# A decoder layer on one core: the end of the cross attention's norm moves from GpSimd to VectorE

## The reference

```
x = x + xattn(layernorm(x), ctx)
q, k, v = relu(query @ Wq + bq), relu(ctx @ Wk + bk), relu(ctx @ Wv + bv)   # 16 heads of 16
probs   = softmax(causal(q k^T / 4))
out     = probs @ v + q
xattn   = (out - mean(out)) * rsqrt(var(out) + 1e-5) * gamma + beta
```

## Time and profile before

| | us |
|---|---|
| median of 3 runs | 1577.68 (1575.25 to 1577.74) |
| the profiled execution, its own time | 1575.13 |
| its span | 1573.4 |
| mean granted clock of TensorE | 0.972 of full speed |

### The profile page before, as it was taken

One profiled execution on the slowest core, in us unless ns is written; L12 is line 12 of the kernel. 1 busy time (PEld: TensorE's weight loads), 2 busy tenths in 40 slices (PEclk: granted clock), 3 DMA queues, 4 the chain that ended last, 5 costly groups with the idle time before them and its releaser, 6 DMA issues. The chain is left out here.

```text
span 1573.4 us, 55175 instructions
## 1 busy us (share of the span) xinstructions
PE 1472.8 (94%) x21214; PEld 1069.1 (68%) x21214; DVE 1085.3 (69%) x3026; ACT 890.6 (57%) x1542; POOL 869.5 (55%) x1172
## 2 busy tenths in 40 slices
PE   5999999999999999986999999999999759999997
PEld 3777777777777777765777677777767536666664
DVE  5667777776767777644566666666666548988986
ACT  2555555555555555543656566665656427777773
POOL 1455555555555455541667776777777724454453
PEclk8999999999999999988999999999999959999998
DMA  5400000000000000003000000000000000000001
GB/s 157 131 2 1 0 0 0 0 0 0 0 0 0 0 0 0 2 2 116 20 19 13 20 13 20 13 17 17 13 20 8 2 1 21 28 34 33 27 34 40
DMA packets 31205, 32.37 MB, mean 21 GB/s; under 512 B 3937, under 2 KB 29602, under 8 KB 31138
## 3 DMA queue, kind: packets, MB, share of 16 engines
q1 hardware_dynamic: 31138, 31.46, 6.5%
HBM read 23.06 MB, written 8.39 MB: 20 GB/s over the span
## 5 line engine op out<-in xcount | busy, mean ns | idle before, releaser
L994 POOL TENSOR_SCALAR_AFFINE_SELECT a_probs_t<-a_probs_t 128x512 f32<-128x512 f32 x256 | 161.8, 666 | 84.1 <-ACT a_probs_t L676 84.1
L1475 DVE TENSOR_REDUCE c_neg_max<-score_banks 128x8 f32<-128x512 f32 (+1 forms) x128 | 116.7, 953 | 101.5 <-PE score_banks L1247 101.4
L1587 POOL TENSOR_SCALAR_AFFINE_SELECT c_probs_t<-c_probs_t 128x512 f32<-128x512 f32 x256 | 153.2, 634 | 34.2 <-ACT c_probs_t L1401 34.1
L1008 POOL TENSOR_TENSOR a_less<-a_attn,a_remote 128x512 f32<-128x512 f32 x32 | 40.7, 1273 | 226.7 <-DVE a_attn L854 226.7
L362 PE MATMUL side_banks<-a_xn_t,a_w_qk 128*128 128x256 f32 x512 | 134.1, 397 | 1.8 <-ACT a_xn_t L621 1.8
L1401 ACT ACTIVATE c_probs_t<-score_banks 128x2048 f32<-128x2048 f32 x64 | 120.3, 1880 | 25.9 <-PE score_banks L1275 25.9
L676 ACT ACTIVATE a_probs_t<-score_banks 128x2048 f32<-128x2048 f32 x64 | 120.2, 1878 | 25.7 <-PE score_banks L520 25.7
L831 DVE TENSOR_REDUCE a_neg_max<-score_banks 128x8 f32<-128x512 f32 (+1 forms) x128 | 116.4, 951 | 13.9 <-PE score_banks L488 13.9
L362 PEld LDWEIGHTS side_banks<-a_xn_t,a_w_qk 128*128 128x128 f32 x512 | 93.4, 197 | 11.7 <-ACT a_xn_t L621 2.2
L2090 POOL TENSOR_TENSOR r_hn<-rz_t,half_hn 128x256 f32<-128x256 f32 x32 | 23.3, 729 | 123.6 <-ACT rz_t L1922 123.6
L631 ACT ACTIVATE a_k_z<-side_banks,a_b_k,row_half 128x256 f32<-128x256 f32 x128 | 61.7, 562 | 47.4 <-PE side_banks L362 47.4
(11 more groups left out here) (255 smaller groups left out, 3939.8 us busy)
## 6 DMA issues: line engine op xcount, KB each, us to landing
x_sb<-in_x SPq DMA_DIRECT2D x32, 256.0 KB, 2.9
c_ctx_in<-in_ctx SPq DMA_DIRECT2D x32, 256.0 KB, 2.7
out<-y SPq DMA_DIRECT2D x32, 256.0 KB, 2.1
w_ih<-in_ffn_w_ih SPq DMA_DIRECT2D x1, 768.0 KB, 6.5
w_hh<-in_ffn_w_hh SPq DMA_DIRECT2D x1, 768.0 KB, 7.3
a_raw_qk<-in_attn_qk_w SPq DMA_DIRECT2D x1, 512.0 KB, 3.6
a_raw_cross<-in_xattn_qk_w SPq DMA_DIRECT2D x1, 512.0 KB, 4.4
b_ih<-in_ffn_b_ih SPq DMA_DIRECT2D x1, 384.0 KB, 6.6
```

What stands on the lines that cost most here:

```text
L994: nc.gpsimd.affine_select(out=probs, in_=probs, pattern=[[0, 4], [1, 128]], compare_op=ALU.is_ge, fill=0.0, base=-1, channel_multiplier=-1 ...
L1475: ins = nc.vector.tensor_reduce(neg_max[:, tt, :].rearrange("p (i s l) -> p i s l", i=4, s=2)[:, :, :, late], all_scores[:, :, :, 128 * (1 ...
L1587: nc.gpsimd.affine_select(out=heads, in_=heads, pattern=[[0, 4], [1, 128]], compare_op=ALU.is_ge, fill=0.0, base=0, channel_multiplier=-1) ...
```

## The change

`out_scale` no longer writes normed, but ends the norm itself: two instructions with three operands (subtract the mean, times gamma) write scaled, and, once `add_beta` and these are done, two more (times one over the deviation, plus x_beta) write x. GpSimd loses `scale_normed`; it gets `add_beta(old)`, one instruction that writes x + beta into the new tile x_beta, between `out_deviation(old)` and `x_deviation(second)`. The tiles normed and shifted go; `add_query` waits for scaled instead of normed.

```diff
             def out_scale(at):
                 dve.wait_ge(norm_scaled, at.count(1, 1))
-                wait(dve, x_done, at.count(1, 0))
-                norm_scale(lambda tt: summed[:, tt, :], normed, out_moments, out_rstd, norm_ready)
+                for tt in range(2):
+                    ins = nc.vector.scalar_tensor_tensor(scaled[:, tt, :], summed[:, tt, :], out_moments[:, tt, 0:1],
+                                                         cross.gamma[:], ALU.subtract, ALU.mult)
+                ins.then_inc(scaled_ready, 1)
+                dve.wait_ge(beta_added, at.count(1, 1))
+                dve.wait_ge(scaled_ready, at.count(1, 1))
+                for tt in range(2):
+                    ins = nc.vector.scalar_tensor_tensor(x_rows(at, tt), scaled[:, tt, :], out_rstd[:, tt:tt + 1],
+                                                         x_beta[:, tt, :], ALU.mult, ALU.add)
+                ins.then_inc(x_done, 1)
...
             def add_query(at):
-                wait(pool, norm_ready, at.count(1, 0))
+                wait(pool, scaled_ready, at.count(1, 0))
...
-            def scale_normed(at):
-                pool.wait_ge(norm_ready, at.count(1, 1))
-                nc.gpsimd.tensor_tensor(scaled[:], normed[:], cross.gamma[:].unsqueeze(1).to_broadcast([128, 2, D]),
-                                        ALU.mult).then_inc(shift_step, 1)
-                pool.wait_ge(shift_step, at.count(2, 1))
-                nc.gpsimd.tensor_tensor(shifted[:], scaled[:], cross.beta[:].unsqueeze(1).to_broadcast([128, 2, D]),
-                                        ALU.add).then_inc(shift_step, 1)
-                pool.wait_ge(shift_step, at.count(2, 2))
-                nc.gpsimd.tensor_tensor(x_pair(at), x_pair(at), shifted[:], ALU.add).then_inc(x_done, 1)
+            def add_beta(at):
+                wait(pool, x_done, at.count(1, 0))
+                nc.gpsimd.tensor_tensor(x_beta[:], x_pair(at), cross.beta[:].unsqueeze(1).to_broadcast([128, 2, D]),
+                                        ALU.add).then_inc(beta_added, 1)
 
             def step(at):
...
                 if old.real:
                     mask_weights(old, 1)
-                if older.real:
-                    scale_normed(older)
                 if old.real:
                     add_query(old)
                 if prev.real:
                     mask_weights(prev, 0)
                 if old.real:
                     out_deviation(old)
+                    add_beta(old)
                 if second.real:
                     x_deviation(second)
```

More of the change, by code:

```diff
@@ L1112, in cross_attention @@
     summed = sb("summed", [128, 2, D])
-    normed = sb("normed", [128, 2, D])
     scaled = sb("scaled", [128, 2, D])
-    shifted = sb("shifted", [128, 2, D])
+    x_beta = sb("x_beta", [128, 2, D])
     k_bank, q_bank, av_bank, back_bank = bank[4:8]
@@ L1132, in cross_attention @@
     sum_step, attn_ready, sum_ready = s("sum_step"), s("attn_ready"), s("sum_ready")
-    norm_step, norm_eps, norm_scaled, norm_ready = s("norm_step"), s("norm_eps"), s("norm_scaled"), s("norm_ready")
-    shift_step, x_done, pool_turn = s("shift_step"), s("x_done"), s("pool_turn")
+    norm_step, norm_eps, norm_scaled, scaled_ready = s("norm_step"), s("norm_eps"), s("norm_scaled"), s("scaled_ready")
+    beta_added, x_done, pool_turn = s("beta_added"), s("x_done"), s("pool_turn")
     pe_turn = s("pe_turn")
@@ L1592, in add_query @@
                 pool.wait_ge(qT_ready, at.count(1, 1))
-                wait(pool, norm_ready, at.count(1, 0))
+                wait(pool, scaled_ready, at.count(1, 0))
                 nc.gpsimd.tensor_tensor(summed[:], attn[:], q_tok[at.par][:], ALU.add).then_inc(sum_ready, 1)
-            def scale_normed(at):
-                pool.wait_ge(norm_ready, at.count(1, 1))
-                nc.gpsimd.tensor_tensor(scaled[:], normed[:], cross.gamma[:].unsqueeze(1).to_broadcast([128, 2, D]),
-                                        ALU.mult).then_inc(shift_step, 1)
-                pool.wait_ge(shift_step, at.count(2, 1))
-                nc.gpsimd.tensor_tensor(shifted[:], scaled[:], cross.beta[:].unsqueeze(1).to_broadcast([128, 2, D]),
-                                        ALU.add).then_inc(shift_step, 1)
-                pool.wait_ge(shift_step, at.count(2, 2))
-                nc.gpsimd.tensor_tensor(x_pair(at), x_pair(at), shifted[:], ALU.add).then_inc(x_done, 1)
+            def add_beta(at):
+                wait(pool, x_done, at.count(1, 0))
+                nc.gpsimd.tensor_tensor(x_beta[:], x_pair(at), cross.beta[:].unsqueeze(1).to_broadcast([128, 2, D]),
+                                        ALU.add).then_inc(beta_added, 1)
             def step(at):
-                prev, old, older, second = at.back(), at.back(2), at.back(3), at.back(-2)
+                prev, old, second = at.back(), at.back(2), at.back(-2)
                 if old.real:
                     mask_weights(old, 1)
-                if older.real:
-                    scale_normed(older)
                 if old.real:
```

## The result

The changed kernel takes 1618.13 us (median of 4 runs, 1617.58 to 1619.69) against 1576.47 us before (1575.00 to 1577.74) in the same comparison: 41.7 us more, ratio 1.0269 (95% interval 1.0255 to 1.0283). The forecast was 1610, the sum behind it +32.9 us.

A forecast was written before the change was run, and what follows sets the result against it. It took TensorE, waiting for GpSimd's second masks in cross attention, to bound the kernel: 37.1 us of waits less 4.2 at the stage's end gave 1608.0, with the median's 2.55 more 1610.6; forecast 1610 us, range 1602 to 1621.

The forecast's parts named there:

- the sum: Cross-attention stage: 37.1 us of added TensorE waits less 4.2 us at the stage's end, +32.9 us.
- The main step: add_beta in GpSimd's queue ahead of the second masks makes TensorE wait 1.25 us more a period, about 17.45 us.
- The part prices: Last pairs of the stage: pair 29 pays 0.82 us for add_beta, pair 30 the full 1.25 us.
- The clock: Rival: TensorE's idle time lowers its clock for a tenth of its stage work, some 51 us more, 1661; 6%.
- the prediction's signs of being wrong: Period of 16.2 to 16.6 us, transposed scores waiting for VectorE instead of masks, or granted clock under 1.00.
- the range: Whole kernel: 1602 us (1.0 us a period) to 1621 us (both upper bounds).
- the room above 1610: Contention and addresses at their bounds: 0.13 + 0.23 us more a period, +10 us, 1620; 7% for either at full size.
- VectorE's part: Four out_scale instructions ahead of row_max take 1.6 to 1.7 us, 0.9 more, costing nothing under GpSimd's delay.
- The rival itself: VectorE decides and GpSimd's delay is swallowed: 0.15 to 0.35 us a period, 1578 to 1584 us; 4%.
- Contention: GpSimd's masks meeting VectorE's small instructions on the maxima: bounds 0 and 0.13 us a period, taken as 0.
- the end of the stage: After the last pair's attn, add_query starts earlier and the shorter norm ends sooner: 4.2 us less.
- The row that the prediction named for it: VectorE's c_xn at 978 ns where GpSimd is busy, beside 0.73 us for a pair of the same form.

The follow-up runs named there:

- Experiment 2: Kernel before plus one unused 128x512 GpSimd instruction between out_deviation and x_deviation, VectorE unchanged: 1614.93 us, ratio 1.0264.
- 1: Changed kernel with add_beta(old) moved right behind add_query(old), no longer between the deviations: 1579.46 us, ratio 1.0036.
- 7: Kernel before plus one unused GpSimd instruction of half size (128x256) between out_deviation and x_deviation: 1594.12 us, ratio 1.0128.
- experiment 8: Kernel before plus two unused 128x512 GpSimd instructions between out_deviation and x_deviation: 1687.50 us, ratio 1.0711.
- experiment 3: Changed kernel with four extra transposes of ident on TensorE in its wait ahead of the second half's values: 1612.48 us, ratio 1.0236.
- experiment 10: Kernel before plus two unused 128x512 GpSimd instructions and twelve extra TensorE transposes in the wait for the masks: 1652.86 us, ratio 1.0492.
- 9: Changed kernel with add_beta behind add_query and x_deviation one step later, behind the second masks; out_scale whole at its place: 1581.75 us, ratio 1.0042.
- experiment 4: Changed kernel with add_beta behind add_query, x_deviation behind the second masks, out_scale at the end of VectorE's step: 1565.05 us, ratio 0.9937.
- experiment 5: Kernel before, arithmetic untouched, with only x_deviation moved one step later, behind the second masks: 1555.21 us, ratio 0.9887.

## Why the prediction was right, and where its sizes were off

*The main step held to the hundredth.* The queue of GpSimd between the moments and the second masks closes a loop through TensorE, and `add_beta` in it costs 1.24 us of every period: the forecast period of 17.45 us is the one measured. Experiment 2 has it with nothing else changed, 1 takes it away by moving one line, 7 and 8 scale it (16.90 and, in the undisturbed periods, 18.69). The part prices are right too. From the opening of a step to its second block of mask matmuls, between which the waiting matmuls of `values` sit, pair 29 takes 3.84 us before and 4.66 after, 0.8 more (0.82 predicted), and pair 30 takes 3.39 and 4.61, 1.2 more (1.25 predicted). The waits are thus 34.7 + 0.8 + 1.2 = 36.7 us, against 37.1 in the sum.

*The clock was the term that the sum lacked.* It stood among the rivals, as a fall for a tenth of the stage at 51 us. It came in addition, and small: five falls of 1.5 us in the profiled execution, 7.5 of the 10 us by which its span grew more than the sum said (43.0 against 32.9). One of the prediction's signs of being wrong, a granted clock under 1.00 in the stage, did show. That the result still lies in the range is in part luck: the room above 1610 stood there for contention and addresses, which cost nothing in the loop, and the clock filled it. Experiments 3 and 10 show the cause: TensorE's idle time in the waits. The same kernels with transposes in the wait, so more work on the same path and the same periods of 17.45 and 18.69 us, have no fall, which rules out a limit on power and a coincidence with the length of the period; experiment 8 has many falls, and 7, with less waiting, none. The transposes shorten both the longest wait and the sum of the waits, so which of the two matters the runs don't tell. Why the falls of the changed kernel come in every fifth period and not in the four between, which look the same, is open as well. The Trainium skill, TensorE: Matmul & The Clock Gate, A second HAM failure mode: psum-queue depth-cycling, describes a bfloat16 kernel in which short idle times between groups of matmuls come often enough to make the clock oscillate between its two levels. The runs agree in kind: waits of 0.7 and three times 0.16 us per 17.45 us went with five falls.

*VectorE's part was mis-sized, and hidden.* I had put the four instructions at 1.6 to 1.7 us; they take 2.0, because the wait between the two pairs costs 0.22 us and each pair takes 0.87 or 0.88 (0.76 by the estimate). The step said that this costs nothing while GpSimd's delay covers it and 0.15 to 0.35 us without it. Uncovered, in experiments 1 and 9, it costs 0.23 us above the 16.21 of the kernel before, inside these bounds; against the 15.57 that TensorE could run at, it is 0.87. So VectorE was a second limit right behind the first. The rival itself, VectorE in place of GpSimd's delay, did not come true: the period is 17.45, not 16.4. Experiments 1 and 9, which take the delay away by hand, end where the rival's price lay (1579 and 1582 us, against 1578 to 1584). In the last step of the stage, where no wait for the masks covers it, the longer `out_scale` did cost 0.5 us. TensorE before, then after:

```profile
1243.62 1.17 PE L1269 MATMUL score_banks<-c_q_f,c_k_z 32*128 32x128 f32 x32 [1.62 <-DVE c_neg_max L1475]
```
```profile
1287.95 1.17 PE L1268 MATMUL score_banks<-c_q_f,c_k_z 32*128 32x128 f32 x32 [2.15 <-DVE c_neg_max L1474]
```

*Contention.* The masks kept their 634 ns, so 0 was right for them. VectorE's two small instructions on the maxima lost 0.3 and 0.4 us to them (0.17 to 0.48 and 0.55 us), which the slack took. At the end of the stage it did cost:

```profile
1303.93 0.70 POOL L1581 TENSOR_TENSOR c_out_rstd<-c_out_var_eps,minus_half 128x2 f32<-128x2 f32 x1
1304.60 1.26 POOL L1605 TENSOR_TENSOR c_x_beta<-x_sb,beta 128x512 f32<-128x512 f32 x1
```
```profile
1304.66 1.87 DVE L1516 SCALAR_TENSOR_TENSOR c_scaled<-c_summed,c_out_moments,gamma 128x256 f32<-128x256 f32 x2 [1.08 <-POOL c_out_rstd L1581]
1306.64 0.88 DVE L1522 SCALAR_TENSOR_TENSOR x_sb<-c_scaled,c_out_rstd,c_x_beta 128x256 f32<-128x256 f32 x2
```

The prediction had `add_beta` run beside VectorE's first two instructions. They took 1.87 us instead of 0.87. Taken singly, the first ran 1.47 us, until 0.27 us after add_beta's end, and the second 0.47, as usual: 1.0 us of the time that they shared was lost. From the last attn (1300.74 + 0.43) to the last write (1306.64 + 0.88) are 6.35 us, against 9.82 before: 3.5 us gained, not 4.2. This is the rule of the Trainium skill that the prediction weighed (SBUF — State Buffer, Who interferes with whom), and the trace agrees with these 1.0 us; the prediction did not apply it in this one place, and experiment 4 met it again. The row that the prediction named for it, c_xn, has only one tensor as input, so it was no example of the rule for two; the rows here and in experiment 4 are.

*The edges.* Between pair 30's waits and the last attn the changed kernel takes 0.7 us more. 0.5 of it is the wait for row_max above; the rest fits TensorE's lower clock, which lasted longer there (`values` of the last pair 1.94 us, 1.64 before). The slots stage of the profiled execution is 2.0 us longer, though the prediction had it unchanged. Runs of one kernel differ by that much (1572.4 to 1578.1 for the kernel before in one comparison), so I give it no cause.

## What to carry to other kernels

An engine that idles for almost a third of a period (GpSimd before: 14.5 of 50 us) can still hold the kernel: look for the instruction that the bottleneck waits for, and count what stands in the queue between that instruction and the event which starts it. The start of the pipeline, where a step is not yet in the queue, shows for nothing what the loop costs; it pointed to the 15.57 us that experiment 5 reached by moving one call. When work moves to another engine, place the new instructions by the gaps of both engines, and fill no gap with an operation that the other blocks.

## What the runs showed of the hardware that was not expected

- TensorE's granted clock went to near half (0.54 to 0.60) for some 3 us at a time in periods in which the engine never waited longer than 0.8 us at once. Transposes that nobody reads, put into the wait, kept it at 1.00 in experiment 3, and in experiment 10, where the wait had been 1.93 us (1687.5 to 1652.9 us).
- A three-operand instruction on VectorE and a GpSimd instruction, both on SBUF, held each other up both ways: 0.87 to 1.87 us on VectorE against add_beta, 2.40 to 2.76 us on GpSimd's four masks, 0.19 to 0.49 us on an addition of 128x2.
